# One VectorE instruction for the maxima of both banks of a score pair

## The reference: what is computed

```python
def _attn(q, k, v, mask):
    scores = jnp.einsum('bqhd,bkhd->bhqk', q, k) / np.float32(np.sqrt(HD))
    scores = jnp.where(mask[:, None, None, :], jnp.float32(-jnp.inf), scores)
    w = jax.nn.softmax(scores, axis=-1)
    return jnp.einsum('bhqk,bkhd->bqhd', w, v)
...
for i in range(NL):
    xn = _adaln(x, noise_emb, n1_w[i], n1_b[i])
    q, k, v = jnp.split(xn @ qkv_w[i].T, 3, axis=-1)
    a = _attn(_rope(q), _rope(k), v, src_mask) @ so_w[i].T
    x = x + a
    ...   # the same with k and v from the context
    x = x + (gelu(xn @ f1_w[i].T + f1_b[i]) @ f2_w[i].T + f2_b[i])
```

## Time and profile before

| | |
|---|---|
| time, median of 3 executions | 3732.65 us (3724.59 to 3735.26) |
| the profiled execution's own time | 3727.94 us |
| its span in the trace | 3726.1 us |
| busy share of the span: PE, DVE, ACT, POOL | 80%, 53%, 51%, 22% |
| mean granted clock of PE | 0.908 of full speed |
| one layer of the loop in the first stack | about 218.5 us |

### The profile page before, as it was taken

How to read it: one execution, slowest core, us unless ns; L and a number is a source line. 1 busy time by engine, 2 the same in 40 slices (tenths; PEclk the granted TensorE clock), 3 DMA queues, 4 the chain that set the end, 5 groups by cost and what they waited for, 6 DMA issues and landing times.

```text
span 3726.1 us, 49832 instructions
## 1 busy us (share of the span) xinstructions
PE 2996.2 (80%) x15209; PEld 990.2 (27%) x15209; DVE 1987.2 (53%) x3503; ACT 1914.4 (51%) x2696; POOL 822.9 (22%) x1339
## 2 busy tenths in 40 slices
PE   6698999986878788787878845878878787888866
PEld 2243333332222222222222211222222222222225
DVE  3313444426557375655837445737465583756624
ACT  4443333334647466564746632746656474665632
POOL 0000444432212222221221221222122122122211
PEclk9898999987989899898989976989999898999987
DMA  1001000001011110100111000111010011101020
GB/s 40 13 32 29 1 1 1 1 12 42 25 30 39 31 38 24 49 25 29 41 31 35 25 13 20 39 31 38 24 49 26 29 40 32 35 26 48 22 111 11
DMA packets 125558, 110.56 MB, mean 30 GB/s; under 512 B 49983, under 2 KB 116077, under 8 KB 125293
## 3 DMA queue, kind: packets, MB, share of 16 engines
q1 hardware_dynamic: 114924, 97.80, 8.9%
q10 hardware_dynamic: 10368, 9.44, 0.8%
HBM read 41.96 MB, written 0.52 MB: 11 GB/s over the span
## 4 chain that ended last, share of the span: by engine, by line
PE 65%; DVE 15%; issue 7%; ACT 6%; POOL 3%; ACTq 2%; SPq 1%; DVEq 0%; DMA 0%; POOLq 0%
PE ps L508 10%; DVE arena L783 7%; PE ps L453 6%; PE ps L482 4%; PE ps L631 3%; PE ps L616 3%; PE ps L574 3%; PE ps L536 3%; PE ps L1435 3%; ACT arena L656 3%; PE ps L560 2%; PE ps L1451 2%; PE ps L525 2%; PE ps L552 2%; PE ps L516 2%
## 5 line engine op out<-in xcount | busy, mean ns | idle before, releaser
L656 ACT ACTIVATE arena<-ps 128x1024 f32<-128x1024 f32 x960 | 936.4, 1024 | 344.7 <-PE ps L482 340.9
L783 DVE TENSOR_REDUCE arena<-ps 128x1 f32<-128x512 f32 x1536 | 967.2, 684 | 206.4 <-PE ps L453 180.4
L508 PE MATMUL ps<-arena 128*32 128x512 f32 x3840 | 512.1, 608 | 20.5 <-ACT arena L656 18.0
L453 PE MATMUL ps<-arena 49*128 49x512 bf16 x1536 | 319.9, 413 | 237.5 <-DVE arena L783 200.6
L482 PE MATMUL ps<-arena 52*128 52x512 bf16 x1920 | 346.1, 386 | 29.0 <-ACT arena L656 25.5
L785 DVE TENSOR_REDUCE arena<-ps 128x3 f32<-128x462 f32 (+1 forms) x576 | 303.3, 580 | 107.4 <-PE ps L460 103.4
L865 POOL TENSOR_TENSOR arena<-arena,zeros 128x16 bf16<-128x16 f32 x192 | 42.2, 220 | 1076.4 <-DVE arena L783 636.6
L453 PEld LDWEIGHTS ps<-arena 49*128 49x128 bf16 x1536 | 75.3, 94 | 588.3 <-DVE arena L783 496.4
L875 POOL TENSOR_TENSOR arena<-arena 128x512 f32<-128x512 f32 x96 | 121.9, 1270 | 451.9 <-ACT arena L688 451.9
L881 POOL TENSOR_TENSOR arena<-arena 128x512 bf16<-128x512 f32 (+1 forms) x84 | 92.4, 1100 | 549.0 <-ACT arena L715 549.0
L803 DVE SCALAR_TENSOR_TENSOR tmp<-tmp,arena,rstd 128x512 f32<-128x512 f32 x72 | 54.1, 752 | 268.8 <-ACT rstd L705 266.5
(11 more groups left out here) (364 smaller groups left out, 4255.3 us busy)
## 6 DMA issues: line engine op xcount, KB each, us to landing
arena<-arena SPq DMA_DIRECT2D x720, 64.0 KB
arena<-we_dram SPq DMA_DIRECT2D x24, 578.5 KB, 8.1
arena<-arena ACTq DMA_DIRECT2D x144, 64.0 KB
w<-weights_dram SPq DMA_DIRECT2D x26, 320.0 KB, 3.0
w<-weights_dram SPq DMA_DIRECT2D x13, 512.0 KB, 3.7
arena<-arena SPq DMA_DIRECT2D x384, 6.0 KB
arena<-arena SPq DMA_DIRECT2D x288, 19.2 KB
w<-weights_dram SPq DMA_DIRECT2D x39, 128.0 KB, 2.2
```

Of the source, the lines that this page charges most:

```text
L453: pe.matmul(s_bank(slot + r), qst[b][rows, idx, P * qt:P * (qt + 1)], kst[b][rows, idx, :], start=True, stop=True).then_inc(s_full, 1 + (z ...
L508: mm = pe.matmul(bank(7)[32 * j:32 * j + 32, :], v, prob[:, slot, j, :], start=(g % 2 == 0 and kt == 0), stop=(a == 0 and g % 2 == 1 and k ...
L656: act.activation(prob[:, chunk_no(b, a, g, kt) % NPROB, 2 * p:2 * p + 2, :], e_bank(slot).rearrange("p (j n) -> p j n", j=2), ACT.Exp, sca ...
L783: op = ve.tensor_reduce(nmax[:, g % 2, r, n:n + 1], s_bank(slot + r), AX.X, ALU.max, negate=True)
```

## The change

In the DVE step of a score pair, where the pair begins in slot 0 or 1 (its two banks lie side by side), one `tensor_reduce` now reads both banks and writes both maxima. It waits until both banks are full, and raises `s_free` by two when it has ended. A pair that begins in slot 2 is done as before. The code of PE, ACT, POOL and SP is the same.

```diff
                 slot, at = z.use("s", it)
                 if n == 0:
                     ve.wait_ge(max_split, floor0(z.ahead("group", it) - 4))
+                if slot + 1 < RING["s"]:
+
+                    ve.wait_ge(s_full, at + 2)
+                    two = bank(slot, 2).rearrange("p (r n) -> p r n", r=2)
+                    if a == 0:
+                        op = ve.tensor_reduce(nmax[:, g % 2, :, n], two, AX.X, ALU.max, negate=True)
+                    else:
+                        op = ve.tensor_reduce(nmax[:, g % 2, :, 3 * n:3 * n + pack(n)],
+                                              two[:, :, 0:pack(n) * CTX].rearrange("p r (i n) -> p r i n", n=CTX),
+                                              AX.X, ALU.max, negate=True)
+                    op.then_inc(s_free, 2 + z.skipped("s", it))
+                    return
                 for r in range(2):
                     ve.wait_ge(s_full, at + r + 1)
```

## The result

The changed kernel takes 4024.9 us (median of 4 executions, 4020.48 to 4031.32) against 3733.95 us for the kernel before (median of 4, one more than above); the ratio is 1.0785, with a 95% interval of 1.076 to 1.0811. It is 291 us slower. The prediction said slower by 155 us, with a range up to 3945: the direction and the late release behind it hold, the size is off by almost half.

The account below looks back on a forecast made before the run. The prediction took PE, working in order and held up by DVE's reductions, to set the pace. Profiled 3727.94 us + 150 of lateness + 8 of clock = 3886; it gave 3888 in the metric, range 3825 to 3945.

Parts of the forecast that it names:

- the late release: Self and cross pairs: the first bank comes back only with the second, 0.535 us later for a self pair.
- prices of the merged instructions: DVE's two-bank reductions: 1219 ns for self pairs, 1116 and 794 ns for cross pairs.
- How much arrives at the end: Whole kernel: of the 192 us of lateness, about three quarters or a little more, 150 us, reach the end.
- lateness read pair by pair: Pairs behind merged pairs: 476 of 606 start late on PE, by 192 us in all.
- the prediction's round: Unbroken burst of self pairs: a merged pair costs 1.22 + 0.06 + 0.43 = 1.71 us, against 1.20 before.
- PE's clock: PE in thinned-out bursts: a fall to half clock costs up to 1.6 us; 8 us taken in all.
- bound from above: PE's weight loads that waited for a reduction: each is late by the whole, 224 us.
- clock rival: PE's clock falls three more times in a layer, 58 us on top and longer waits, 3950 to 4030; chance 0.05.
- in single places only: Sign on PE: the trace so far showed short idles making the clock go back and forth only there.
- mostly swallowed: PE's other waits, 20 us a layer, could cover the 16 us of lateness; 3745 to 3830; chance 0.08.
- faster: DVE's 692 fewer instructions save 48 us if the first bank's release doesn't matter; 3685; chance 0.03.
- nothing measurable: Whole kernel: DVE's saving and the lateness meet, 3722 to 3744; chance 0.03.

Follow-up runs that it names:

- late_release: Kernel before, nothing merged, but in slots 0 and 1 both banks are given back only by the second reduction; 4014.5 us, ratio 1.0764.
- wait_both: Kernel before, but in slots 0 and 1 the first reduction waits until both banks are full, each bank released by its own reduction; 3744.6 us, 1.0055.
- merge_unheld: Kernel before with merging only at 17 places of a layer where the next pair started late enough or none follows directly; 3741.8 us, 1.0032.
- before_early: Kernel before, but PE writes a self pair's first bank as soon as that bank is free; 3725.6 us, ratio 0.9992.
- merge_calm: Kernel before with merging only in six of a layer's 16 score groups, where the change left the clock nearly alone; 3846.0 us, ratio 1.0319.
- merge_cross: Kernel before with merging for cross pairs alone, 202 of the 692; 3816.9 us, ratio 1.0237.
- merge_restless: Kernel before with merging only in the ten of 16 score groups where time at half clock had grown; 3922.8 us, ratio 1.0519.
- heavy pair: One extra float32 matmul before each pair of ten score groups, in the kernel before (3799.6 us, 1.0185) and in the changed kernel (4027.5 us, 1.0799).
- warm pair: Two extra matmuls before every self pair, in the kernel before (3935.1 us, 1.0553) and in the changed kernel (4177.9 us, 1.1213).
- after_heavy: Changed kernel with one extra float32 matmul on the whole array before each pair of ten score groups; 4027.5 us, ratio 1.0799.

## Why the prediction was wrong

**What held.** The mechanism: late_release reproduces the whole loss with no instruction merged, and wait_both, merge_unheld and before_early show that the wait for both banks costs 18 us, the merged instruction where nobody waits 12, and that an earlier first matmul wins nothing as long as the banks come back early. The prices of the merged instructions are right to 6 ns, and ACT's and POOL's busy times moved by less than 8 us.

**The step "How much arrives at the end"** failed: it took 150 of the 192 us of lateness read pair by pair, on the argument that PE's other waits, some 20 us a layer, would swallow a fifth. No such share was swallowed. In merge_calm five groups kept their clock (batch 1 self group 0 and 2, batch 0 self group 3, group 2 of both cross attentions; the time at half clock in them changed by 1.2 us at most). For these the lateness read from the kernel before was 14.6 + 14.2 + 13.1 + 5.7 + 11.3 = 58.9 us over twelve layers, and measured were 13.6 + 17.5 + 16.5 + 6.8 + 13.0 = 67.4, a factor of 1.14. By that factor the release is worth 192 x 1.14 = 219 us. What lifts it above 1 is most likely a term that the prediction's round left out, the 0.10 us by which the merged reduction starts late. In full that term would give more: the lateness was read to the next pair's weight load, and with 0.10 us added it is some 242 us. Read to the matmul, which is what the array waits for, it is 225 us with the 0.10, and 70 for the five groups, of which the measured 67.4 are nearly all. PE is followed in order by ACT, and ACT waited longer for PE (496.3 us before line 656 instead of the 344.7 of the earlier trace rows), so ACT's lateness came from PE and gave PE no slack.

**The step "PE's clock"** failed by the largest factor: it took 8 us, and priced even the rival at 58. Measured are 263 us more at half clock, in 36 more falls, on average three in a layer, where one more in a layer had been the most that I took into the sum. A fall was priced at up to 1.6 us, read over 3.4 us; the stretches at half clock last 951 / 121 = 7.9 us on average, and one more costs some 2 us. What a microsecond at half clock costs is read in several ways. Within one and the same kernel, executions with a lower mean clock take longer: fitted over 97 executions of all kernels here, each against its own kernel's mean, 0.27 us for one. The untouched group gave 0.22 over all layers and 0.33 in the two picked out. And the rest of the change, 291 - 219 = 72, is 0.27 x 263; this is no reading of its own, since 219 comes from five groups. The same two prices, 1.14 for lateness and 0.27 for half clock, give for merge_cross 49 x 1.14 + 0.27 x 132 = 92 (measured 88), for merge_restless 119 x 1.14 + 0.27 x 248 = 203 (194) and for merge_calm 73 x 1.14 + 0.27 x 59 = 99 (117).

One part alone, the loss going with lateness only, is the rival that the whole kernels leave standing. The 16 groups of the traces of the change, merge_calm, merge_restless and merge_cross speak against it. A fit of each group's added time by its lateness (read to the matmul) and its added time at half clock gives 1.12 and 0.28, close to the two prices above. With lateness alone the groups scatter by 4.9 us around the fit, with both by 3.2.

So the 291 us are about 220 of late release and about 70 of clock, where the prediction had 150 and 8. The division is good to some 20 us, as the misses of the small sums show. The pairs with extra matmuls lie further off: by the same prices the heavy pair would stand 219 + 0.27 x 143 = 258 us apart (measured 228) and the warm pair 219 + 0.27 x 214 = 277 (243), probably because those matmuls hide in the longer waits of the change and not in those of the kernel before. What made the clock fall is the same late release: late_release, where nothing else differs, has a mean clock of 0.876. That it does so by thinning out PE's work in the bursts is argued; after_heavy fits, since more PE work there brought much of the clock back and paid for itself.

**The bounds and the rivals.** The bound from above, 224 us, was priced as an upper end, yet with the round's missing 0.1 us the release alone came close to it; the high end of the range, 3945, held 20 us of clock and had to hold 70. The clock rival (0.05), 3950 to 4030, held the result: it counted three more falls in a layer, as found, and put 58 us on them, near the 70 found. That it reached 4030 was in part luck, for the rest was an unpriced "longer waits behind them", and what filled it was the lateness that arrived whole. I gave it too small a chance because its sign stood "in single places only". The Trainium skill ("TensorE: Matmul & The Clock Gate", the second failure mode) speaks of short idles between matmul groups that make the clock go back and forth; the traces here agree, with 121 falls in place of 85 and 263 us more at half clock, where the array's idles in the burst above became 1.4 us in place of 0.8. The rivals "mostly swallowed", "faster" and "nothing measurable" fell.

**A better version.** Neither a merged variant nor the early first matmul beats the kernel before: the nearest, before_early, is at 0.9992 with an interval that holds 1.

## What to carry to other kernels

Before two instructions on a shared ring are merged, ask what the first one's release let start. Here at most 0.07 us saved in an instruction cost a hand-over that had been hidden, 0.5 us and more where the next pair waited. In this kernel lateness read pair by pair on an in-order engine that others wait for arrived nearly whole; other waits of that engine are no cushion if they hang on its own output. And a change that adds many short waits to PE is to be priced twice, once for the waits and once for the clock, at 0.2 to 0.35 us for each one at half clock in this kernel.

## What the runs showed of the hardware that was not expected

- A reduction over two PSUM banks of 1024 float32 elements took 1225 ns, one over 512 took 686: the bank's edge costs nothing in its duration. But it started 527 ns after the matmuls' start, where a reduction of one bank started after 424, and one of one bank that waits for both after 458.
- The spread between executions of one kernel goes with PE's clock (correlation 0.85 over the 97). Those of the kernel before ranged from 3719.92 us at a mean clock of 0.913 to 3733.64 at 0.906, on one chip.
- Useless matmuls can be free. A float32 matmul of 128 x 128 by 128 before each of 600 pairs left the time of the changed kernel where it was (4027.5 against 4024.9 us) and made one group 1.69 us shorter in one layer, with the clock at 1.00 in place of 0.81. The bf16 ones on 49 rows, 1536 of them and before self pairs alone, did not lift the clock (0.881) and cost 153 us; whether it is their type, their rows or their place that matters is not shown.
